# Attention scores on the tensor engine: masks added by 32x32 tiles, the value product taken per quad of heads, and one ring of score buffers for two passes

## What is computed

```python
Q = rope(x_norm @ w_q.T + b_q); K = rope(ctx @ w_k.T + b_k); V = ctx @ w_v.T + b_v
scores = einsum('bhqd,bhkd->bhqk', Q, K) / sqrt(8)
scores = where(mask == 0, -1e9, scores)      # mask: 1 x 1 x 256 x 256
attn = softmax(scores, axis=-1)
ctx = einsum('bhqk,bhkd->bhqd', attn, V)
out = x + ctx_heads_joined @ w_o.T + b_o
```

## Time and profile before

| what | value |
|---|---|
| time, median of 3 runs | 351.27 us (349.31 to 352.09) |
| the profiled execution's own time | 353.96 us |
| its span in the profile | 351.9 us |
| PE busy | 311.0 us, 88% of the span |
| DVE, ACT, POOL busy | 221.3, 160.5, 155.9 us |
| first pass A on PE | 26.7 us |
| attention with both passes | slots 11 to 31, to about 120 us |
| pass B alone | to about 149 us |
| expert units | from about 149 us to the end |

### The profile page before, as it was taken

The page is one execution under the profiler, slowest core; times in us unless marked ns, Lnnn a source line. Parts: engine busy times, 40 slices in busy tenths (PEclk is TensorE's granted clock), DMA queues, the critical chain, the costliest instruction groups (busy, mean ns, idle before and its releaser), DMA issues.

```text
span 351.9 us, 4644 instructions
## 1 busy us (share of the span) xinstructions
PE 311.0 (88%) x1570; PEld 196.9 (56%) x1570; DVE 221.3 (63%) x485; ACT 160.5 (46%) x278; POOL 155.9 (44%) x174
## 2 busy tenths in 40 slices
PE   3549889999999999988879987996998996999993
PEld 1323454454444445455657765685775775877771
DVE  4716676445567634478696585467669358766663
ACT  1100034443444556564645553844455753554441
POOL 6264023122111413229378772455754456455551
PEclk9955559999999999999999998998999998999999
DMA  7798917317220202020202020020000000001001
GB/s 199 216 153 197 223 28 172 69 47 163 33 62 2 60 4 63 0 60 0 61 0 61 2 60 0 0 61 0 0 4 0 0 2 0 0 0 32 0 2 30
DMA packets 10247, 18.17 MB, mean 52 GB/s; under 512 B 1328, under 2 KB 7024, under 8 KB 9712
## 3 DMA queue, kind: packets, MB, share of 16 engines
q1 hardware_dynamic: 8496, 11.59, 14.8%
q10 hardware_dynamic: 1728, 6.29, 6.7%
HBM read 15.19 MB, written 2.62 MB: 51 GB/s over the span
## 4 chain that ended last, share of the span: by engine, by line
PE 55%; DVE 13%; DMA 12%; POOL 6%; ACT 4%; issue 4%; SPq 4%; POOLq 0%; ACTq 0%; DVEq 0%
PE psum L1032 51%; DMA qk_scratch<-parts 6%; DMA ctxk<-ctx_tok 3%; DVE early L1002 2%; DVE xn L898 2%; DVE early L1008 2%; DMA pvT<-mask_k 2%; DMA big<-qk_scratch 1%; POOL big L546 1%; ACT early L686 1%; POOL parts L546 1%; DVE stats L727 1%; SPq L383 1%; SPq L368 1%; ACT L686 1%
## 5 line engine op out<-in xcount | busy, mean ns | idle before, releaser
L1002 DVE TENSOR_TENSOR early<-early,psum 128x512 f32<-128x512 f32 x64 | 43.7, 683 | 48.1 <-ACT early L686 48.0
L686 ACT ACTIVATE early<-psum 128x512 f32<-128x512 f32 x64 | 38.4, 599 | 65.8 <-PE psum L1032 65.8
L546 POOL TENSOR_TENSOR parts<-early,parts 128x512 fp32r<-128x512 f32 x32 | 41.3, 1291 | 49.7 <-ACT parts L678 49.5
L1032 PE MATMUL psum<-xs,ws 128*128 128x512 f32 x192 | 56.5, 431 | 0.0
L1032 PE MATMUL psum<-xs,big 128*128 128x512 f32 x192 | 55.1, 423 | 0.0
L983 DVE TENSOR_REDUCE negmax<-psum 128x4 f32<-128x1024 f32 x32 | 39.1, 1222 | 23.6 <-PE psum L1032 23.5
L648 ACT ACTIVATE early<-psum 128x1024 f32<-128x1024 f32 x32 | 32.8, 1024 | 40.6 <-PE psum L1032 40.5
L1008 DVE TENSOR_TENSOR early<-early,psum 128x512 f32<-128x512 f32 x64 | 44.0, 687 | 4.2 <-POOL big L546 1.6
L1032 PE MATMUL psum<-maskb,id 128*128 128x512 bf16 x128 | 43.7, 427 | 0.4 <-DVE negmax L983 0.4
L1032 PEld LDWEIGHTS psum<-big 32*128 32x128 f32 (+1 forms) x256 | 21.3, 206 | 37.9 <-issue 30.8
L1032 PEld LDWEIGHTS psum<-xs,big 128*128 128x128 f32 x192 | 36.4, 193 | 8.2 <-issue 0.7
(11 more groups left out here) (180 smaller groups left out, 446.9 us busy)
## 6 DMA issues: line engine op xcount, KB each, us to landing
raw<-experts ACTq DMA_DIRECT2D x12, 512.0 KB, 3.7
big<-qk_scratch SPq DMA_DIRECT2D x24, 128.0 KB
qk_scratch<-parts SPq DMA_DIRECT2D x16, 128.0 KB, 2.7
big<-qk_scratch SPq DMA_DIRECT2D x16, 64.0 KB
early<-sel SPq DMA_DIRECT2D x2, 512.0 KB, 8.1
ropet<-rope SPq DMA_DIRECT2D x2, 256.0 KB, 5.1
ctxk<-ctx_tok SPq DMA_DIRECT2D x1, 512.0 KB, 11.1
out<-x_in SPq DMA_DIRECT2D x2, 256.0 KB, 3.1
```

The source lines that it names most:

```text
L546: nc.gpsimd.tensor_tensor(hs(n)[:, 1, :], h32[:, n % 2, :], hs(n)[:, 0, :].bitcast(F32), ALU.subtract).then_inc(lo_ready, 1)
L686: nc.scalar.activation(sg[:, n % 2, :], psum[:, n % 2, :], ACT.Silu).then_inc(silu_ready, 1)
L1002: nc.vector.tensor_tensor(sg[:, n % 2, :], sg[:, n % 2, :], psum[:, 2 + n % 2, :], ALU.mult).then_inc(up_read, 1)
L1032: return nc.tensor.matmul(o, w, r, start=start, stop=stop, skip_group_check=True)
```

## The change

The masks. Each two-bank mask is now written by eight products of a 32x32 identity block with 32 rows of the mask. In bank r the block of rows 32g goes to partitions 32c with c = (g + r) mod 4, so that the eight products use eight different tiles of the array. For this `maskb` holds every mask twice, the second time with its blocks turned by one (`turned_blocks`, on the host). The mask by query is loaded at the start (the bytes that both masks had before), and the mask by key at the head of `late_loads`; DVE converts it in `masks_by_key()`, placed after slot 6.

The value product. It is done per quad (two pairs, four heads) in every second slot, with the four heads side by side in the inner loop, into half a bank, and ACT evicts each quad (128x256) rather than every second one (128x512).

The banks. Passes A and B share three two-bank buffers (banks 0 to 5) in the order of `WINDOWS`. A window waits for the reader of the window three places back. The value product has bank 6, and the small tasks of the slots have bank 7 alone: each waits until the one before it has been read. In the expert units, small tasks use 6 and 7 in turn.

```diff
+def slot_windows(s):
+    windows = [("max", s)] if s < A_SLOTS else []
+    return windows + ([("exp", s - B_START)] if 0 <= s - B_START < A_SLOTS else [])
...
-            return psum[:, 6 + misc_index(task) % 2, :]
-        BANK_PV = 4
-        BANK_NOTFULL = 5
+            k = misc_index(task)
+            return psum[:, BANK_MISC if k < SLOT_USES else BANK_PV + (k - SLOT_USES) % 2, :]
+        BANK_PV = 6
+        BANK_MISC = 7
+        WINDOWS = [w for s in range(SLOTS) for w in slot_windows(s)]
+        def window_bank(kind, at):
+            return 2 * (WINDOWS.index((kind, at)) % 3)
...
-            sp.dma_start(maskq_i[:, 0, :, :], mask_q).then_inc(in_mask, 16)
-            sp.dma_start(maskq_i[:, 1, :, :], mask_k).then_inc(in_mask, 16)
+            sp.dma_start(mask_i[:, :, :, :], mask_q).then_inc(in_mask, 16)
...
             def late_loads():
+                sp.wait_ge(masks_ready, 1)
+                sp.dma_start(mask_i[:, :, :, :], mask_k).then_inc(in_mask_k, 16)
                 x_batches(2, B, in_xrest)
...
-                        act.wait_ge(pv_done, t - 3)
+                        act.wait_ge(pv_done, (t - 4) // 2 + 1)
...
-                if t >= 4 and t % 4 == 0:
+                if t >= 2 and t % 2 == 0:
+                    quad = t // 2 - 1
+                    act.wait_ge(pv_done, quad + 1)
...
+                    nc.scalar.copy(pvT[:, quad % QUADS, :], psum[:, BANK_PV, 0:S]).then_inc(pv_evicted, 1)
...
+            def masks_by_key():
+                dve.wait_ge(in_mask_k, 16)
+                nc.vector.tensor_scalar(maskb[:, 1, :, :, :], mask_i[:, :, :, :], 0.0, MASKED, ALU.is_equal,
+                                        ALU.mult).then_inc(mask_k_ready, 1)
...
+                if s == PAIRS - 2:
+                    masks_by_key()
...
-                if k >= 2:
-                    prev = uses[k - 2]
+                before = k - 1 if k < SLOT_USES else k - 2
+                if k == SLOT_USES:
+                    pe.wait_ge(pv_evicted, B * QUADS)
+                if before >= 0 and k != SLOT_USES:
+                    prev = uses[before]
...
+                def window(kind, at):
+                    w = WINDOWS.index((kind, at))
+                    if w >= 3:
+                        before, reads = WINDOWS[w - 3]
+                        pe.wait_ge(maxes_read if before == "max" else exps_done, reads + 1)
+                    bank, m = 2 * (w % 3), int(kind == "exp")
+                    for g in range(4):
+                        rows = slice(32 * g, 32 * (g + 1))
+                        for r in range(2):
+                            c = (g + r) % 4
+                            mm(psum[32 * c:32 * (c + 1), bank + r, :], id16[rows, rows],
+                               maskb[rows, m, r, :, :].rearrange("p t k -> p (t k)"), True, False)
+                    return bank
...
-                    for r in range(2):
-                        mm(psum[:, bank + r, :], id16[:, :], maskb[:, 0, :, :].rearrange("p t k -> p (t k)"), True, False)
+                    bank = window("max", s)
...
-                if t >= 1:
-                    p = t - 1
-                    pb, quad, quarter = p // PAIRS, p // 2, p % 2
-                    pe.wait_ge(exps_done, p + 1)
+                if t >= 1 and t % 2 == 0:
+                    quad = t // 2 - 1
+                    pb = quad // QUADS
+                    pe.wait_ge(exps_done, 2 * quad + 2)
...
+                    if quad >= 1:
+                        pe.wait_ge(pv_evicted, quad)
                     for k in range(QT):
-                        for r in range(2):
+                        for g in range(4):
```

More of the change, by code:

```diff
@@ L134, in unit_tasks @@
     return tasks
+SLOT_USES = sum(1 for s in range(SLOTS) for t in slot_tasks(s) if t[0] in MISC_READER)
 def misc_index(task):
@@ L981, in _ @@
                     dve.wait_ge(scores_max, s + 1)
[L982 removed]
+                    bank = window_bank("max", s)
                     nc.vector.tensor_reduce(negmax[:, b % 2, :, :].rearrange("p t (r j) -> p r t j", r=2)[:, :, :, j],
@@ L1184, in _ @@
                     if t == 0:
-                        pe.wait_ge(maxes_read, B_START)
-                    if s == A_SLOTS:
-                        pe.wait_ge(maxes_read, A_SLOTS)
-                    bank = b_bank(t)
-                    reads = t if t >= 1 and b_bank(t - 1) == bank else t - 1
-                    if reads >= 1:
-                        pe.wait_ge(exps_done, reads)
-                    for r in range(2):
-                        mm(psum[:, bank + r, :], id16[:, :], maskb[:, 1, :, :].rearrange("p k q -> p (k q)"), True, False)
+                        pe.wait_ge(mask_k_ready, 1)
+                    bank = window("exp", t)
                     if b_j == 0:
@@ L1202, in _ @@
                     last.then_inc(scores_exp, 1)
-                if t >= 1:
-                    p = t - 1
-                    pb, quad, quarter = p // PAIRS, p // 2, p % 2
-                    pe.wait_ge(exps_done, p + 1)
-                    if p % PAIRS == 0:
+                if t >= 1 and t % 2 == 0:
+                    quad = t // 2 - 1
+                    pb = quad // QUADS
+                    pe.wait_ge(exps_done, 2 * quad + 2)
+                    if quad % QUADS == 0:
                         pe.wait_ge(misc_dve, misc_reads(("vproj", pb)))
-                    if p % 4 == 0 and p >= 8:
-                        pe.wait_ge(pv_evicted, p // 4 - 1)
+                    if quad >= 1:
+                        pe.wait_ge(pv_evicted, quad)
                     for k in range(QT):
-                        for r in range(2):
-                            g = 2 * quarter + r
-                            h = 2 * (p % PAIRS) + r
-                            last = mm(psum[32 * g:32 * (g + 1), BANK_PV + (quad // 2) % 2, S * (quad % 2):S * (quad % 2 + 1)],
+                        for g in range(4):
+                            p, r = 2 * quad + g // 2, g % 2
+                            h = 4 * (quad % QUADS) + g
+                            last = mm(psum[32 * g:32 * (g + 1), BANK_PV, 0:S],
                                       vaug[:, pb % 3, k, VW * h:VW * h + 32], probs[:, p % 4, r, k, :],
@@ L1306, in selectors, with turned_blocks @@
     return m.reshape(P, UNITS * P)
+def turned_blocks(mask):
+    rows = mask.reshape(QT, P, S).transpose(1, 0, 2).reshape(4, P // 4, QT, S)
+    return np.stack([rows[(np.arange(4) + r) % 4] for r in range(2)], axis=2).reshape(P, 2, QT, S)
 def kernel(x, ctx_1024, mask_1x1xSxS2_ik0, mask_BxS2_bk0, L0_xattn_w_q, L0_xattn_b_q, L0_xattn_w_k, L0_xattn_b_k,
@@ L1341 @@
         "x": a(x).reshape(T, D), "ctx_t": a(ctx_1024).reshape(T, D).T, "ctx_tok": a(ctx_1024).reshape(T, D),
-        "mask_q": mask.reshape(QT, P, S).transpose(1, 0, 2), "mask_k": mask.T.reshape(QT, P, S).transpose(1, 0, 2),
+        "mask_q": turned_blocks(mask), "mask_k": turned_blocks(mask.T),
         "pad": a(mask_BxS2_bk0).reshape(1, T), "small": small, "rows": rows, "experts": experts,
```

51 lines of the change are left out of this document (20 added, 31 removed).

## The result

The changed kernel takes 368.35 us (median of 4 runs, 365.79 to 371.36), the kernel before beside it 351.42: a ratio of 1.044 [1.038, 1.050]. I had forecast 344 with a range of 337 to 366, so the sign was wrong and the time lies 2.3 us outside the range. The profiled execution of after took 371.36, the longest of the four, with a span of 369.3. Medians are over all executions of a kernel; ratios leave out those that took over 1.5% more than its quickest.

The account below looks back on a forecast made before the run. PE was taken to bound the kernel from 68.7 to 148.9 us, loads before that. Terms -11.9 - 5.2 + 5.2 + 4.5 = -7.4 took the profiled 353.96 to 346.6, for the median 344 us; range 337 to 366.

Parts of the forecast that it names:

- priced slots 16 to 42 at the full clock: Attention slots: PE work saved is time won, 11.9 us in slots 16 to 31 and 5.2 in 32 to 42.
- the clock at full from about 58: Sign listed for the forecast: PE granted its full 2.4 GHz from about 58 us on.
- the third rival: PE stays at 1.2 GHz: up to slot 17, 352 us (chance 0.10); up to slot 31, 376 us (0.05).
- Masks: Each window's mask: eight tile products in one round, 0.38 us from mask to scores, 0.15 less per window.
- The second rival: Masks: row groups writing one bank take turns, four rounds, 1.0 us per mask, 370 us in all; chance 0.14.
- The rule of the Trainium skill: Masks: different row tiles cannot use the same PSUM bank at the same time; masks would take four rounds.
- Value product: Slots 16 to 42: a quad takes 0.99 us, as a pair did, saving 0.50 per slot; 1.9 of waits back.
- One bank: Small tasks of the slots wait for the reader of the one before, and PE stands still: 5.2 us lost.
- the ring: Score buffers of passes A and B: lets PE run further ahead of the reader; no term of its own.
- Loads: Late `mask_k` load delays `ctxk` by 2.6 us and slot 7's maximum to 44.4; slot 16 shifts 4.5 us.
- The sum: Whole kernel: -11.9 - 5.2 + 5.2 + 4.5 = -7.4 us.

Follow-up runs that it names:

- experiment 1: The changed kernel with each window's masks written again by two products of the whole 128x128 array: 352.11 us, ratio to the kernel before 0.998.
- experiment 9: The kernel before with masks by eight 32x32 products and the second mask loaded late; value product by pairs, two small-task banks: 352.02 us, ratio 0.999.
- experiment 6: The kernel before with only the value product done per quad in every second slot, in its old banks: 342.01 us, ratio 0.970.
- experiment 10: The kernel before with small masks, second mask loaded late, and value product per quad in its old banks: median 356.0 us, five executions from 344.83 to 364.67.
- experiment 4: The changed kernel with the value product per pair in every slot again, masks still small: 364.92 us (357.89 to 372.51).
- experiment 11: The kernel before with only the small tasks of the slots put into one bank, bank 7: 362.48 us, ratio 1.026.
- experiment 5: The changed kernel with whole 128x128 mask products and both masks loaded and converted at the start: 349.06 us, ratio 0.989.
- experiment 8: The kernel before with only the second mask fetched late, as 512 KB ahead of the late loads, and converted in slot 6: 354.72 us, ratio 1.006.

## Why the prediction was wrong

**The step that failed** is the one that priced slots 16 to 42 at the full clock ("the clock at full from about 58"). I did have the clock as the third rival, at 0.10 for 352 us and 0.05 for 376. After did something between the two: half the clock to slot 16, then on and off to slot 42. From the rows: after slot 16 the mean grants of 0.79 over 53.3 us and 0.63 over 33.7 are 22.4 and 24.9 us at half, 47.3 in all. What takes 2.55 us at full takes 4.43 at half, so 42% of these, 20 us, is the clock's. Another 3.3 is the difference at slot 16 between after (76.32) and experiment 1 (73.00), which had the full clock from 59.8 us on. Sum 23. The experiments give 19 to 24: after is 16.2 above experiment 1, in which masks stand on PE that cost more by 41 x 0.19 = 7.8 us at the local price, and by 2.7 to 5.6 as experiment 9 measured it. (The 7 us at half that experiment 1 has itself are not counted.)

The evidence was in my own rows: 12.35 of 13.00 us busy and granted half. I used them to price half a clock and gave the state itself 15%, because before got the clock with its first slots around the query projection. The rows say that a busy PE is not enough, and no more: the stretch from 27 to 40 has half the clock in every kernel of the study, with whole masks too. The question that I didn't put was what keeps the clock up after 54. Experiments 6, 9 and 10 answer it for a kernel with two banks for small tasks: whole masks with quads keep it, small masks with pairs nearly so, small masks with quads do not.

**What the falls follow.** In after the clock falls at 93, 120, 141 and 165 us, each time behind waits of PE for DVE at the small tasks. Waits ahead of the first two, with a mask at the price of half the clock after the first (0.62 long, 0.41 before):

```profile
91.89 0.71 PE L1051 MATMUL psum<-sm,ctxT 128*128 128x128 f32 x4 [0.68 <-DVE ctxn L841]
...
93.45 0.62 PE L1051 MATMUL psum<-maskb,id 32*32 32x512 bf16 x8
...
119.54 0.66 PE L1094 MATMUL psum<-id,pvT 128*128 128x128 f32 x4 [1.99 <-DVE ctxn L841]
```

Such a pair of waits, 0.68 us each around the transposes of slot 20, stands in experiments 1, 4 and 11 as well. With quads the clock falls behind it: in experiment 1 from 90.5 to 97.5, in after from 93 to 107, and in experiment 5, which has the pair too, from 85 to 88.5. With pairs it stays full, with whole masks (11) and with small ones (4). In experiment 6, quads without the single bank, it stays full there too. So the single bank, which I priced by PE's idle time alone, also has a part in the clock's fall; how many of the 19 to 24 us are its part no run separates. That the masks decide as well is seen in the time until the clock is back: in after, with small masks, 14, 14 and 20 us, with whole masks 7 (experiment 1) and 3.5 and 13.5 (experiment 5).

**Masks.** Forecast 0.38 from mask to scores, measured 0.34. The second rival, four rounds for row groups that write one bank, is out: the eight products of a window take 0.34 us, where 1.0 was its price. The rule of the Trainium skill that the prediction cites ("TensorEngine Tiling (Array Packing)", section Restrictions and Gotchas) does not hold here, where the row groups write different partitions of the bank. Of the 0.19 a window, worth 7.8 us, experiment 9 kept 5.6 in the profiled spans (354.0 to 348.4) and 2.7 in the medians.

**Value product.** Forecast 0.99 a quad, measured 1.00. My terms for it, 26 slots at 0.50 less 1.9 of waits, are 11 us. Experiment 6 measured 10.

**One bank.** Forecast 5.2, of which the places I listed make only 4.8. Alone it costs 9, with quads and the ring 7. The size of a wait was right (1.1 forecast and 0.97 measured in slot 17, 0.8 and 0.68 in slot 20), but I counted the wait behind the key projection in slot 17 alone, and left out slot 9 (1.00 us, at 50.16 in experiment 11) and slot 0. And the time lost from slot 16 on is 2 us more than the waits of PE that I can name.

**Loads.** Forecast 4.5 at slot 16. Experiment 1 has 4.3 there, released by the stack's DMA (0.61 us of idle) as forecast. In after it is 7.6, and no DMA sets it: PE is busy without a pause from 54.33 on, at half the clock. Without the late load (experiment 5) slot 16 comes at 67.73, 5.3 earlier than in experiment 1, while late load and bank alone cost 0.9 and 1.5 (experiments 8 and 11); why together they cost more I did not follow up. `ctxk` was late by 1.2 us, not 2.6 (ACT's unpacking starts at 48.63 where it was 47.39). `mask_k` landed at 43.15 (42.5 forecast) and the maximum of slot 7 followed at once:

```profile
43.15 0.69 DVE L775 TENSOR_SCALAR maskb<-pvT 128x1024 bf16<-128x1024 int32 x1 [5.34 <-DMA pvT<-mask_k]
43.76 1.22 DVE L997 TENSOR_REDUCE negmax<-psum 128x4 f32<-128x1024 f32 x1
```

It ended at 44.98, 44.4 forecast. On the end of the kernel the load costs 2 to 3 us.

**The sum** without the clock: quads -10, bank and ring +7, load +3, and masks -2.7 to -7.8, is -3 to -8, where the prediction had -7.4. Of the miss of 24 us the clock is 19 to 24; the rest, up to 5, hangs on what the small masks are worth and stays open. That bank and ring together come near the forecast is partly luck: the bank alone costs 9 where I had 5.2, and I had put the ring at nothing.

What stays open: what the single bank's waits and the small products each have of the clock's loss, whether it is the rows, the columns or the number of tiles in use that the clock answers to, and why equal executions of experiment 10 get 0.84 to 0.91 of it.

## What to carry to other kernels

Packing small products side by side gives the time that the tiles promise, but on a PE-bound kernel it pays only while the granted clock holds, so read the clock of every stretch in the row after the busy share, before summing prices at the full one. Check that clock against a price, the distance of two starts, since the line can miss the start of an execution. Where a stretch of before has a busy PE and half the clock, count half the clock among the likely states of a changed stretch that looks like it, and count a new wait of PE as a place where it can fall. Take a change apart before judging it: one of its parts was worth 3%.

## What the runs showed of the hardware

- With PE equally busy, 512 added columns a window on the whole array took after from 368 to 358 us, and on one 32x32 tile to 409.
- Eight bf16 products of 32x32 tiles with 512 columns, in four row and four column groups, writing two banks, took 0.34 us at the full clock and 0.56 at half, where two whole products take 0.53 and 0.96.
- The same two waits of PE of 0.68 us each, in slot 20, were followed by half the clock in the profiled executions with value products by quads (after and experiment 1), and not in those with pairs (experiments 4 and 11).
- A profile can give the full clock for a stretch that had half: experiment 1 shows 1.00 from 27 to 40 us and a mean of 0.978, but took 0.96 us from mask to scores there, as before did at 0.50.
